# Selective scan stage: both channel halves in one VectorE instruction, the next step's scan ahead of this step's product, four input buffers, one activation table set

## The reference

```python
xz = x @ in_proj_w.T
xc, z = jnp.split(xz, 2, axis=-1)
xt = conv1d(pad(xc), conv_w)                      # 4 taps, each channel by itself
xc = silu(xt + conv_b)
dbc = xc @ x_proj_w.T                             # 8 columns dt, 16 columns B, 16 columns C
delta = softplus(dt @ dt_proj_w.T + dt_proj_b)
A = -exp(A_log)
dA = exp(delta[..., None] * A)                    # one decay for each token, channel, state
dBu = (delta * xc)[..., None] * Bm[:, :, None, :]
h[t] = dA[t] * h[t-1] + dBu[t]                    # along the 256 tokens of a sequence
y[t] = sum over the 16 states of h[t] * C[t]
y = (y + xc * D) * silu(z)
return y @ out_proj_w.T                           # added to x
```

## Time and profile before

| | |
|---|---|
| median of 3 runs | 3349.98 us (3343.85 to 3350.4) |
| profiled execution, its own time | 3351.04 us |
| its span, first to last instruction | 3349.3 us |
| mean granted TensorE clock | 0.872 of 2.4 GHz |
| busy: PE, DVE, ACT, POOL | 2545.6, 2050.8, 1395.3, 1884.4 us |
| first scan starts, last scan starts | 2343.7 us, 2820.5 us |

### The profile page before, as it was taken

One profiled execution on the slowest core, in us unless ns is written; L12 is line 12 of the kernel. 1 busy time (PEld: TensorE's weight loads), 2 busy tenths in 40 slices (PEclk: granted clock), 3 DMA queues, 4 the chain that ended last, 5 costly groups with the idle time before them and its releaser, 6 DMA issues. The chain is left out here.

```text
span 3349.3 us, 69215 instructions
## 1 busy us (share of the span) xinstructions
PE 2545.6 (76%) x24495; PEld 1645.0 (49%) x24514; DVE 2050.8 (61%) x6095; ACT 1395.3 (42%) x2956; POOL 1884.4 (56%) x2224
## 2 busy tenths in 40 slices
PE   3438975879994658899978999572887885999772
PEld 2228873556883434555545555460333332555462
DVE  6862225773334545588835787314999999788613
ACT  2202212322221315266642666335666662466433
POOL 4776772574774212299952134573778887124564
PEclk8679996869997879799987999795899998899886
DMA  9207973222996632010001011223121120111133
GB/s 374 80 3 187 221 184 80 74 82 73 227 223 190 221 88 105 14 20 19 14 2 21 20 27 40 67 69 110 51 79 74 51 91 21 19 23 35 46 92 97
DMA packets 222727, 294.18 MB, mean 88 GB/s; under 512 B 36704, under 2 KB 179583, under 8 KB 216288
## 3 DMA queue, kind: packets, MB, share of 16 engines
q1 hardware_dynamic: 168544, 245.65, 23.6%
q0 software_dynamic: 47616, 39.44, 6.3%
q10 hardware_dynamic: 6272, 5.24, 0.6%
HBM read 181.88 MB, written 107.12 MB: 86 GB/s over the span
## 5 line engine op out<-in xcount | busy, mean ns | idle before, releaser
L4093 PE MATMUL l3am_y<-l3am_hc,ident 128*128 128x512 f32 x512 | 284.5, 640 | 78.3 <-DVE l3am_hc L3982 77.2
L3753 POOL TENSOR_TENSOR l3am_db<-l3am_du,l3am_bs 128x512 f32<-128x512 f32 x256 | 318.0, 1271 | 45.6 <-DVE l3am_hh L3974 44.8
L3974 DVE TENSOR_TENSOR_SCAN l3am_hh<-l3am_dA,l3am_db 128x512 f32<-128x512 f32 x256 | 300.7, 1214 | 21.2 <-ACT l3am_dA L3883 11.8
L1200 POOL TENSOR_TENSOR l2a_pT<-l2a_pT,kept 128x512 int32<-128x512 int32 x224 | 278.2, 1280 | 46.0 <-ACT l2a_pT L1406 46.0
L3045 POOL DMA_INDIRECT l0f_table<-l0f2e_y,l0f2e_idx x128 | 178.8, 1397 | 77.9 <-issue 33.6
L3045 POOL DMA_INDIRECT l0f_table<-l0f1e_y,l0f1e_idx x128 | 179.5, 1402 | 68.4 <-issue 32.5
L1287 DVE CUSTOM_DVE_ANT_0 l2a_junk<-l2a_s,addend 128x256 f32<-128x256 f32 x486 | 178.2, 421 | 61.3 <-PE l2a_s L1523 46.7
L1873 POOL DMA_INDIRECT l0f_rows<-l0f1r_row,l0f1r_idx x160 | 163.8, 1024 | 73.2 <-issue 51.1
L4093 PEld LDWEIGHTS l3am_y<-l3am_hc,ident 128*128 128x128 f32 x512 | 96.0, 200 | 205.1 <-DVE l3am_hc L3982 143.7
L3883 ACT ACTIVATE l3am_dA<-l3am_dl,l3am_al 128x512 f32<-128x512 f32 x256 | 167.3, 682 | 58.5 <-POOL l3am_dl L3742 29.7
L1280 DVE TENSOR_REDUCE l3f1a_mx<-l3f1a_s 128x2 f32<-128x512 f32 x243 | 156.4, 685 | 40.4 <-PE l3f1a_s L1523 31.4
(11 more groups left out here) (840 smaller groups left out, 6918.3 us busy)
## 6 DMA issues: line engine op xcount, KB each, us to landing
l3am_bs<-l3a_b SPq DMA_DIRECT2D x32, 1024.0 KB, 6.7
...
l3f_rows<-blank SPq DMA_DIRECT2D x8, 1440.0 KB, 11.8
```

Source lines behind the costliest of these rows:

```text
L1200: self.nc.gpsimd.tensor_tensor(t, t, self.kept[:, f // 8 % 2, :].unsqueeze(1).to_broadcast([P, 2, 2 * P]), ALU.mult).then_inc(self.cut_g, 1)
L3753: G.tensor_tensor(db[j][n % 2][:, :], du[j][k % 2][:, :], bs[s // QUARTER][:, s % QUARTER, :], ALU.mult).then_inc(db_ready[j], 1)
L3974: V.tensor_tensor_scan(hh[j][n % 2][:, :], dA[j][n % 2][:, :], db[j][n % 2][:, :], 0.0, ALU.mult, ALU.add).then_inc(h_ready, 1)
L4093: T.matmul(yb[j][:, :], c.ident[:, :], hc[j][n % 2][:, :], start=(s == 0), stop=(s == N - 1)).then_inc(summed, 1)
```

## The change

Only `mamba` changes (and a helper `pair`, which makes a tensor of two PSUM banks). The two halves j of `dA` now lie side by side in one pair of banks, and those of `db`, `du`, `hh` and `hc` side by side in one SBUF tensor, so one DVE instruction of 1024 elements scans both halves and one multiplies both with C; one POOL instruction makes both halves of `db`. The first token of the second half is made a restart of the recurrence like the other sequence starts (`edges`). `db` has four buffers, `hh` three, `dA` and `hc` two as before. On DVE the scan of step n+1 stands ahead of the product of step n. On PE `spread_c(n + 1)` stands ahead of both accumulations of step n. On POOL `gate_output` moves from s = 0 to s = 2. On ACT the table set that holds both exponential and logarithm is asked for behind the Silu activations. The cut diff:

```diff
+    def pair(self, name):
+        return self.ctx.enter_context(self.nc.psum_tensor(f"{self.name}_{name}", [P, 1024], F32))
...
-        zs, xs, dl, du = ([rows_of(f"{n}{j}") for j in range(CC)] for n in ("zs", "xs", "dl", "du"))
-        db, hh, hc = ([rows_of(f"{n}{j}") for j in range(CC)] for n in ("db", "hh", "hc"))
+        zs, xs, dl = ([rows_of(f"{n}{j}") for j in range(CC)] for n in ("zs", "xs", "dl"))
+        DB, HH = 4, 3
+        du = rows_of("du", [P, CC, GT])
+        db, hh, hc = ([ph.sb(f"{n}{i}", [P, CC * GT]) for i in range(r)] for n, r in (("db", DB), ("hh", HH), ("hc", 2)))
...
-        dA = [[ph.bank(f"dA{j}{i}") for i in range(2)] for j in range(CC)]
+        dA = [ph.pair(f"dA{i}") for i in range(2)]
...
@@ -3747,11 +3754,11 @@
                     g.wait_ge(du_ready, CC)
                 if s % QUARTER == 0:
                     g.wait_ge(loaded[s // QUARTER], 16 * (k + 1))
-                for j in range(CC):
-                    if n >= 2:
-                        g.wait_ge(h_ready, 2 * n - 3 + j)
-                    G.tensor_tensor(db[j][n % 2][:, :], du[j][k % 2][:, :], bs[s // QUARTER][:, s % QUARTER, :], ALU.mult
-                                    ).then_inc(db_ready[j], 1)
+                if n >= DB:
+                    g.wait_ge(h_ready, n - DB + 1)
+                G.tensor_tensor(db[n % DB][:, :].rearrange("p (j t) -> p j t", j=CC), du[k % 2][:, :, :],
+                                bs[s // QUARTER][:, s % QUARTER, :].unsqueeze(1).to_broadcast([P, CC, GT]), ALU.mult
+                                ).then_inc(db_ready, 1)
 
             def gate_output(k):
                 for j in range(CC):
...
                     inputs(n + 1)
-                if s == 0 and k >= 1:
+                if s == 2 and k >= 1:
                     gate_output(k - 1)
                 if k + 1 < GROUPS:
                     if s in (9, 11):
...
                 a.wait_ge(conv_done, CC * k + 2)
                 A.activation(xs[1][k % 2][:, :], mb[:, :], ACT.Silu, bias=cb[:, 1:2]).then_inc(xs_ready, 1)
+                A.preload_act_table_set("natural_log_exp_and_others")
 
             def read_dbc(k):
...
@@ -3877,10 +3885,10 @@
                 k, s = divmod(n, N)
                 if s == 0:
                     a.wait_ge(edge, CC * (k + 1))
+                if n >= 2:
+                    a.wait_ge(h_ready, n - 1)
                 for j in range(CC):
-                    if n >= 2:
-                        a.wait_ge(h_ready, 2 * n - 3 + j)
-                    A.activation(dA[j][n % 2][:, :], dl[j][k % 2][:, :], ACT.Exp, scale=al[:, j, s:s + 1]
+                    A.activation(dA[n % 2][:, halves[j]], dl[j][k % 2][:, :], ACT.Exp, scale=al[:, j, s:s + 1]
                                  ).then_inc(dA_ready, 1)
 
             a.wait_ge(weights, 176)
...
@@ -3966,20 +3974,23 @@
                                        op0=ALU.mult, op1=ALU.mult).then_inc(scaled, 1)
                 V.tensor_scalar(gain[:, lo:hi], y[:, 0:n], 1.0, None, ALU.add).then_inc(scaled, 1)
 
-            def scan(n, j):
-                v.wait_ge(dA_ready, 2 * n + j + 1)
-                v.wait_ge(db_ready[j], n + 1)
-                if n >= 2:
-                    v.wait_ge(hc_ready, 2 * n - 3 + j)
-                V.tensor_tensor_scan(hh[j][n % 2][:, :], dA[j][n % 2][:, :], db[j][n % 2][:, :], 0.0, ALU.mult, ALU.add
+            def scan(n):
+
+                v.wait_ge(dA_ready, CC * (n + 1))
+                v.wait_ge(db_ready, n + 1)
+                if n >= HH:
+                    v.wait_ge(hc_ready, n - HH + 1)
+                V.tensor_tensor_scan(hh[n % HH][:, :], dA[n % 2][:, :], db[n % DB][:, :], 0.0, ALU.mult, ALU.add
                                      ).then_inc(h_ready, 1)
 
-            def outputs(n, j):
-                v.wait_ge(h_ready, 2 * n + j + 1)
+            def outputs(n):
+                v.wait_ge(h_ready, n + 1)
                 v.wait_ge(c_done, n + 1)
                 if n >= 2:
-                    v.wait_ge(summed, 2 * n - 3 + j)
-                V.tensor_tensor(hc[j][n % 2][:, :], hh[j][n % 2][:, :], cbk[:, :], ALU.mult).then_inc(hc_ready, 1)
+                    v.wait_ge(summed, CC * (n - 1))
+                V.tensor_tensor(hc[n % 2][:, :].rearrange("p (j t) -> p j t", j=CC),
+                                hh[n % HH][:, :].rearrange("p (j t) -> p j t", j=CC),
+                                cbk[:, :].unsqueeze(1).to_broadcast([P, CC, GT]), ALU.mult).then_inc(hc_ready, 1)
 
             def gather(k):
                 v.wait_ge(summed, N * CC * (k + 1))
...
             for j in range(CC):
                 v.wait_ge(du_ready, j + 1)
-                V.memset(dl[j][0][:, SEQ:SEQ + 1], EDGE).then_inc(edge, 1)
+                V.memset(dl[j][0][:, edges[j]], EDGE).then_inc(edge, 1)
+            scan(0)
             for n in range(STEPS):
                 k, s = divmod(n, N)
-                for j in range(CC):
-                    scan(n, j)
+                if n + 1 < STEPS:
+                    scan(n + 1)
                 if s == 0 and k >= 1:
                     gather(k - 1)
-                for j in range(CC):
-                    outputs(n, j)
+                outputs(n)
                 if s == 13 and k >= 1:
                     add(k - 1)
             gather(GROUPS - 1)
...
             def spread_c(n):
                 k, s = divmod(n, N)
                 if s == 0:
                     pe.wait_ge(parts_ready, k + 1)
                 if n:
-                    pe.wait_ge(hc_ready, CC * n)
+                    pe.wait_ge(hc_ready, n)
                 T.matmul(cbk[:, :], sel[:, s, :], parts[k % 2][:, :], start=True, stop=True).then_inc(c_done, 1)
 
             def accumulate(n, j):
                 k, s = divmod(n, N)
-                pe.wait_ge(hc_ready, CC * n + j + 1)
+                pe.wait_ge(hc_ready, n + 1)
                 if s == 0 and k:
                     pe.wait_ge(yy, CC * k - 1 + j)
-                T.matmul(yb[j][:, :], c.ident[:, :], hc[j][n % 2][:, :], start=(s == 0), stop=(s == N - 1)
+                T.matmul(yb[j][:, :], c.ident[:, :], hc[n % 2][:, halves[j]], start=(s == 0), stop=(s == N - 1)
                          ).then_inc(summed, 1)
 
             def output(k):
...
@@ -4122,10 +4133,10 @@
             pe.wait_ge(silu_z, CC)
             for n in range(STEPS):
                 k, s = divmod(n, N)
-                accumulate(n, 0)
                 if n + 1 < STEPS:
                     spread_c(n + 1)
-                accumulate(n, 1)
+                for j in range(CC):
+                    accumulate(n, j)
                 if k + 1 < GROUPS:
                     if s in (0, 1, 2, 3):
                         xz(k + 1, s)

```

More of the change, by code:

```diff
@@ L3648, in mamba @@
         EDGE = 1e30
+        edges = (slice(SEQ, SEQ + 1), slice(0, GT, SEQ))
         def rows_of(n, shape=None, dt=F32):
@@ L3674, in mamba @@
         mb, cbk = ph.bank("misc"), ph.bank("c")
-        dA = [[ph.bank(f"dA{j}{i}") for i in range(2)] for j in range(CC)]
+        dA = [ph.pair(f"dA{i}") for i in range(2)]
         yb = [ph.bank(f"y{i}") for i in range(CC)]
-        first_xz, first_conv, first_dt = (mb, dA[1][1], *yb), (mb, dA[0][1]), (mb, cbk)
+        halves = [slice(j * GT, (j + 1) * GT) for j in range(CC)]
+        first_xz, first_conv, first_dt = (mb[:, :], dA[1][:, halves[1]], yb[0][:, :], yb[1][:, :]), (
+            mb[:, :], dA[1][:, halves[0]]), (mb[:, :], cbk[:, :])
         weights, made, padded, selected, turned_taps, rates, negated = (
@@ L3689, in mamba @@
         loaded = [ph.sem(f"loaded{q}") for q in range(4)]
-        db_ready = [ph.sem(f"db{j}_ready") for j in range(CC)]
-        dA_ready, h_ready, c_done, hc_ready, summed, yy, y_ready, o_done, o_free = (
-            ph.sem(s) for s in ("dA_ready", "h_ready", "c_done", "hc_ready", "summed", "yy", "y_ready", "o_done",
+        db_ready, dA_ready, h_ready, c_done, hc_ready, summed, yy, y_ready, o_done, o_free = (
+            ph.sem(s) for s in ("db_ready", "dA_ready", "h_ready", "c_done", "hc_ready", "summed", "yy", "y_ready", "o_done",
                                 "o_free"))
@@ L3711, in _ @@
                     if k >= 1:
-                        sp.wait_ge(db_ready[1], N * (k - 1) + QUARTER * (q + 1))
+                        sp.wait_ge(db_ready, N * (k - 1) + QUARTER * (q + 1))
                     sp.dma_start(bs[q][:, :, :], b_rows[k % 2][QUARTER * q:QUARTER * (q + 1), :].partition_broadcast(P)
@@ L3737, in steps_by_inputs @@
                     g.wait_ge(dl_ready, CC * k + j + 1)
-                    G.tensor_tensor(du[j][k % 2][:, :], dl[j][k % 2][:, :], xs[j][k % 2][:, :], ALU.mult
+                    G.tensor_tensor(du[k % 2][:, j, :], dl[j][k % 2][:, :], xs[j][k % 2][:, :], ALU.mult
                                     ).then_inc(du_ready, 1)
@@ L3741, in steps_by_inputs @@
                     hold(g, c.mark_g, du_ready, CC * k + j + 1)
```

(26 more changed lines are left out.)

2 lines of the change are left out of this document (1 added, 1 removed).

## The result

| | median of runs | span of the profiled run | mean granted clock |
|---|---|---|---|
| before | 3349.37 us (3343.85 to 3350.4, 4 runs) | 3349.3 us | 0.872 |
| after | 3523.68 us (3522.57 to 3529.8, 4 runs) | 3527.0 us | 0.858 |

The change makes the program slower: ratio 1.0526, 95% interval 1.0511 to 1.0541, or 174 us. The forecast was 3487 in a range of 3455 to 3535.

What follows compares the result with a forecast made beforehand. DVE was taken to bound the kernel before; in the change, stalls from the chain through PE, ACT and POOL add time. 3351 + 114 (stalls less merging gain) + 22 (PE's clock) = 3487 us, range 3455 to 3535.

Steps and rivals of the forecast that it cites:

- The merged instructions: DVE scans and products of 1024 elements: step 3.32 us instead of 3.43, 14 us gained; POOL's merged input about 2.47.
- The moved scan: DVE order: cover for the product-PE-ACT-decays chain falls from 6.8 to 3.23 us; stalls 21.6 a group, together + 114.
- two projections: Steps s = 1 to 4: round of 5.36 us against 3.23 stalls every second step, 2 x 2.1 = 4.3 us a group.
- convolution: Read at s = 6: two taps instead of one product, 0.85 more on PE; a stall of 2.7 us.
- Silus: At s = 8 the last Silu waits for the second convolution; round 7.3 us, a stall of 4.1.
- first split: `split_rows` at s = 9: x_proj result, ACT copy, POOL split, then input of step 11; a stall of 2.0 us.
- second split: After `dt`, s = 10, 11: reads, conversion, POOL subtraction and input of step 13, round 8.8 us; a stall of 5.6.
- group's start: Decays at the group's start wait for POOL's step sizes, now 1.21 us; a stall of 1.8 in the change.
- PE's clock: PE returns from long waits near half clock, lengthening a round by up to 2.6 us; taken as + 22 us.
- The rival of the cold PE: Waits of 2 us also slow PE, six or seven rounds a group: 75 us, total 3530 to 3550; chance 0.12.
- The table loads: Fourteen ACT loads of 1.28 us in softplus: given nothing, worth 18 us if they stood on the path.
- The fourth `db` buffer: At the first split it doesn't help, since POOL's input stands behind the split in POOL's order; stall 2.0 us.

Runs made afterwards that it cites:

- The first experiment: The changed kernel with only DVE's order put back to scan n, then product n, merged instructions kept: 3360.91 us, ratio 1.0041.
- PE's piece first: The changed kernel with PE's preparation for the next group ahead of the row of C and both accumulations: 3361.67 us, ratio 1.0034.
- PE kept busy: The changed kernel plus eleven PE products of zeros per group but the last, where PE would wait: 3484.66 us, ratio 1.0414.

## Why the prediction was right, and what was mis-sized

**The sum of DVE's waits explains the time.** In the change 192.4 + 2.6 us at scans and products, 15.5 at the add and 4.3 at the gather, 214.8 in all; before 21.2 + 2.8 + 3.3 + 1.5 = 28.8. That is 186 more, less 128 x 0.12 = 15 for the shorter step: 171, against 174 measured.

**The merged instructions: right in size, wrong in owner.** The step is 3.31 (forecast 3.32), scan 2.20 (2.19), product 1.11 (1.13), POOL's input 2.35 (2.47). The first experiment shows that this pitch needs the scan ahead.

**The moved scan: right.** The cover is one scan and one product, the chain through PE, ACT and back is longer, and both ways out of it (the old order on DVE, or PE's piece first) give back about 160 us. Stall by stall, in us a group (the last column is the first of the two groups shown):

| | forecast | change | PE kept busy |
|---|---|---|---|
| two projections | 4.3 | 3.47 + 3.50 | 1.95 + 1.94 |
| convolution | 2.7 | 4.07 | 2.85 |
| Silus | 4.1 | 3.94 | 3.94 |
| first split | 2.0 | 1.91 | 1.92 |
| dt | 0.3 | 0.42 | 0.42 |
| second split | 5.6 | 6.67 | 6.69 |
| add | 0.8 | 2.27 | 2.26 |
| group's start | 1.8 | 3.02 | 1.33 |
| sum | 21.6 | 29.3 | 23.3 |

**PE's clock: the term that was mis-sized.** "I take + 22", said the prediction, with only the longest wait and some of those of 3.4 us to bring the clock down. In an ordinary group of the change six rounds come back slow: the four accumulation passes take 3.23 to 3.45 us instead of 1.88 at 2707.71, 2717.92, 2748.29, 2762.23, 2771.64 and 2782.86, behind waits of 2.91, 2.90, 2.16, 7.00, 2.16 and 4.88. So waits of 2.2 to 2.9 us, to which the forecast gave nothing, brought the clock down too. What that costs has two measures. Keeping PE busy gave back 36 us net of the zeros' own time, with some rounds still slow. And the second of its two groups shown, at 0.98 of the clock, takes 77.38 us against 85.33: 8.0 a group, seven times 56. That group's stalls add up to 21.7 (1.95 + 1.94, 2.85, 3.94, 1.92, 0.42, 4.98, 2.34, 1.33), as the forecast's 21.6 do, and its length is near the 76.6 that the forecast had ahead of its term for the clock. The table's last line says nearly the same, 7 x 7.7 = 54. So the clock cost 36 to 56 us, about twice what was taken; the forecast's 137 less 22, with these in their place, is 151 to 171 of the 174.

Most of what a group still lacks is small: 16 x 3.31 + 1.9 + 29.3 = 84.2 of 85.3, and the rest is 0.24 in which a product waits for the row of C, and the 0.08 that each of the waits in brackets leaves out.

The rival of the cold PE gave 3530 to 3550, and the time lies 6 us under that and 37 over the forecast: in size the rival came closer, and on this point its mechanism was the right one. It had six or seven slow rounds a group if waits of 2 us also bring the clock down, and there are six. What it had too high is the price: 1.65 us a round, against 8.0 / 6 = 1.3. Two of the signs that the prediction named came out larger than it said: a group of 85.3 us (76 to 80), and 192.4 us of idle time ahead of the scan (130 to 170). Both would lie inside without the 8.0 us a group. That 3524 is inside the range is owed to the room left at its top for a colder PE. The bottom of the range doesn't come out as stated: stalls a tenth shorter, 19.4 instead of 21.6, give + 99 by the prediction's own sum, 3450, and not + 105; and at its top + 180 is 3531, not 3535.

The prediction took the kernel on the Trainium skill's page "TensorE: Matmul & The Clock Gate" (HAM oscillation), which comes back slow on every tile, as a rule for this rival. That was stretched: the waits there are 3 to 5 us. Here all 12 rounds of the stage behind waits over 4.1 us were slow, which agrees, but so were most behind 2.05 to 3.2, and in all 49 of the 128.

**The group's start: right size, wrong cause.** I put it to POOL's step sizes. What the trace shows is ACT's reading of the turned rows, which waits 5.78 us for PE's transpose of s = 14 ahead of the decays of the group's start:

```profile
2774.77 0.87 PE L4053 MATMUL l3am_misc<-ident,l3am_xn 128*128 128x128 f32 x4
...
2775.68 0.78 ACT L3813 ACTIVATE l3am_xnT<-l3am_misc,l3am_lnb,l3am_lnw 128x512 f32<-128x512 f32 x1 [5.78 <-PE l3am_misc L4053]
...
2776.36 1.29 ACT L3891 ACTIVATE l3am_dA<-l3am_dl,l3am_al 128x512 f32<-128x512 f32 x2
```

It is one more piece in the same chain. **The table loads**, put at nothing, were nothing. **The fourth `db` buffer**, said not to help, didn't: only when POOL's written order was moved too did its waits go.
